# Routed token rows: scattered by expert ahead of time and loaded as whole rows, instead of gathered by an index list

## The reference

```python
def _swiglu(x, w13_, w2_):
    gu = x @ w13_.T
    g, u = jnp.split(gu, 2, axis=-1)
    return jax.nn.silu(g) * u @ w2_.T
scores = jax.nn.softmax(x @ gate_w.T, axis=-1)        # 2048 tokens, 16 experts
topk_w, topk_ids = lax.top_k(scores, 6)
topk_w = topk_w / (topk_w.sum(-1, keepdims=True) + 1e-20)
combine = jnp.einsum('tk,tke->te', topk_w, jax.nn.one_hot(topk_ids, E, dtype=topk_w.dtype))
# out = sum over experts of combine[:, e] * swiglu(x, w13[e], w2[e])  (hidden width 352)
#       + swiglu(x, sw13, sw2)                         (shared, hidden width 704)
x = x + jnp.tanh(g_ffn[0]) * out
```

## Time and profile before

| | |
|---|---|
| median of 3 runs | 1436.95 us (1435.53 to 1438.42) |
| profiled execution: span from first to last instruction | 1435.5 us |
| busy: PE / PEld | 1349.9 us (94%) / 1210.6 us (84%) |
| busy: POOL / DVE / ACT | 949.3 us (66%) / 787.5 us (55%) / 730.9 us (51%) |
| DMA | 149.13 MB, mean 104 GB/s |
| chain that ended last: PE | 65% of the span |
| stage A / shared tiles / routed tiles, about | 0 to 490 / 490 to 700 / 700 to 1425 us |

### The profile page before, as it was taken

How to read it: one execution, slowest core, us unless ns; L and a number is a source line. 1 busy time by engine, 2 the same in 40 slices (tenths; PEclk the granted TensorE clock), 3 DMA queues, 4 the chain that set the end, 5 groups by cost and what they waited for, 6 DMA issues and landing times.

```text
span 1435.5 us, 32257 instructions
## 1 busy us (share of the span) xinstructions
PE 1349.9 (94%) x8480; PEld 1210.6 (84%) x8481; DVE 787.5 (55%) x1364; ACT 730.9 (51%) x1317; POOL 949.3 (66%) x671
## 2 busy tenths in 40 slices
PE   6897998997898899999999999999999999999996
PEld 2686887887888799999998989989889988899885
DVE  6878898898989854653333333333333333333331
ACT  5898897898889464343332333323333333332321
POOL 0588898898988747887456665566645666546632
PEclk8899999999999999999999999999999999999999
DMA  4120122222242365645455435555445544454432
GB/s 137 38 74 31 53 67 96 67 73 91 75 146 72 133 129 106 142 84 141 83 141 145 131 63 144 139 147 137 104 94 137 141 135 104 95 147 131 76 68 36
DMA packets 65042, 149.13 MB, mean 104 GB/s; under 512 B 16976, under 2 KB 17616, under 8 KB 62656
## 3 DMA queue, kind: packets, MB, share of 16 engines
q0 software_dynamic: 31024, 62.10, 22.9%
q1 hardware_dynamic: 33392, 81.21, 17.5%
q10 hardware_dynamic: 560, 4.98, 1.0%
HBM read 101.50 MB, written 48.99 MB: 105 GB/s over the span
## 4 chain that ended last, share of the span: by engine, by line
PE 65%; DVE 3%; issue 1%; POOL 0%; ACT 0%; DVEq 0%; POOLq 0%; ACTq 0%
PE bank L1719 19%; PE bank L1699 19%; PE bank L1700 18%; PE bank L1687 3%; PE bank L1710 3%; DVE hs L1172 1%; PE bank L1604 1%; PE bank L1590 1%; PE bank L1602 0%; POOL hc L949 0%; DVE sc L1226 0%; PE bank L1665 0%; DVEq L1375 0%; DVE xl L1363 0%; DVE du L1186 0%
## 5 line engine op out<-in xcount | busy, mean ns | idle before, releaser
L949 POOL TENSOR_TENSOR hc<-hs,crow 128x512 f32<-128x512 f32 x254 | 322.6, 1302 | 91.8 <-DVE hs L1172 84.6
L1699 PE MATMUL bank<-w,xh 128*128 (+1 forms) x1088 | 368.7, 340 | 7.6 <-issue 4.2
L1015 POOL DMA_INDIRECT out_x<-ys,aid x104 | 171.2, 1646 | 275.0 <-issue 215.7
L1700 PE MATMUL bank<-w,xh 128*128 (+1 forms) x1088 | 351.2, 323 | 0.0
L1172 DVE TENSOR_TENSOR_SCAN hs<-dA,bank 128x512 f32<-128x512 f32 x256 | 295.8, 1208 | 47.9 <-PE bank L1604 32.0
L1719 PE MATMUL bank<-w,ah 128*128 (+1 forms) x816 | 264.7, 405 | 2.7 <-DVE al L1399 2.7
L1399 DVE TENSOR_TENSOR al<-bank,ah 128x384 fp32r<-128x384 f32 x136 | 75.8, 557 | 331.0 <-ACT ah L862 283.2
L1699 PEld LDWEIGHTS bank<-w,xh 128*128 128x128 f32 x1088 | 204.3, 188 | 35.9 <-issue 32.1
L1700 PEld LDWEIGHTS bank<-w,xh 128*128 128x128 f32 x1088 | 206.4, 190 | 2.3
L868 ACT COPY ys<-bank 128x512 f32<-128x512 f32 x136 | 79.9, 587 | 195.9 <-PE bank L1719 191.5
L1700 PE MATMUL bank<-w,xl 128*128 (+1 forms) x544 | 175.9, 323 | 0.0
(11 more groups left out here) (184 smaller groups left out, 2051.7 us busy)
## 6 DMA issues: line engine op xcount, KB each, us to landing
wraw<-in_wall SPq DMA_DIRECT2D x16, 2176.0 KB
crow<-c_rows SPq DMA_DIRECT2D x64, 256.0 KB, 3.3
xt<-token_rows_turned SPq DMA_DIRECT2D x32, 256.0 KB
out_x<-ys POOLq DMA_DIRECT2D x32, 256.0 KB
wraw<-in_wall ACTq DMA_DIRECT2D x2, 2176.0 KB
token_rows<-rowb SPq DMA_DIRECT2D x4, 1028.0 KB
xrow<-in_x SPq DMA_DIRECT2D x4, 1024.0 KB, 7.0
out_x<-xrow SPq DMA_DIRECT2D x4, 1024.0 KB, 4.9
```

The costliest lines, as they stand in the source:

```text
L949: nc.gpsimd.tensor_tensor(hc[:, j, :], hs[:, j, :], crow[:, n % 4, :], ALU.mult).then_inc(hc_done, 1)
L1015: pool.indirect_dma_start(out_rows, bass.IndirectOffsetOnAxis(ap=aid[:, s:s + 1], axis=0), ys[:, s, :], None, bounds_check=TOKENS - 1, oob ...
L1699: nc.tensor.matmul(gate_bank[:, 0:I], xx, columns(w, off + ww + k * 2 * I, I), start=first, stop=last)
L1700: mm = nc.tensor.matmul(up_bank[:, 0:I], xx, columns(w, off + ww + k * 2 * I + I, I), start=first, stop=last)
```

## The change

The token lists and the gathers go. A buffer `expert_rows` in DRAM has a region of 17 x 128 rows for each expert. While the shared tiles run, each batch's finished rows (values, 16 weights, token number, spare) are loaded into SBUF (`srow`, two buffers) and POOL scatters each row of 532 floats to its place in the region of each of its six experts: 96 indirect DMAs, and 16 more that put padding rows behind each expert's last, four a tile in tiles 2 to 29. In the routed stage SP loads each tile as 128 whole neighbouring rows by two DMAs: `xs` (512 values) and `tail` (weights and token number). PE still turns the rows.

SP waits ahead of the first such load for all 112 scatters. SP no longer fetches weights in the routed stage: `wraw` is doubled, and ACT issues the fetch of the set after next right behind its own half of the split, as five DMAs. DVE has no index for the gather to copy, and takes the token number from `tail` instead of from a list by a column number that it first has to load into a register.

```diff
-AHEAD = 5
-FIRST_ROWS = {NS - 3: (NS, NS + 1), NS - 2: (NS + 2,), NS - 1: (NS + 3, NS + 4)}
+TAIL = ROW - H
+IDCOL = TAIL - 2
+REGION = (TT + 1) * P
+PADS = E * REGION
+SCATTERS = TOPK * TT + E
+SCATTERS_AT = dict.fromkeys(range(2, 30), 4)
...
# SP
             def fetch(e):
-                at_least(sp, wl_done, e)
-                sp.dma_start(wraw[:], wall[bass.ds(e, 1)].rearrange("a p c -> p (a c)")).then_inc(raw_in, 16)
+                shared_set(sp, e, raw0)
+
+            def batch_rows(b):
+                if b == 0:
+                    sp.wait_ge(wl_done, 1)
+                if b == 1:
+                    sp.wait_ge(turned_stored, 16 * NB)
+                    sp.wait_ge(base_stored, 16 * NB)
+                sp.wait_ge(rows_stored, 16 * (b + 1))
+                sp.wait_ge(wts_stored, 16 * (b + 1))
+                if b > 1:
+                    sp.wait_ge(listed[b - 2], 16 * TOPK * TC)
+                sp.dma_start(srow[b % 2][:], rows_v[b]).then_inc(srow_in[b % 2], 16)
+
+            def expert_load(t, s):
+                if not (isinstance(t, int) and t < NS + 4):
+                    apart(sp, xt_turned, t - 3, "sp")
+                    apart(sp, aid_done, t - 3, "sp")
+                first = sp.value_load(meta[0:1, 4, bass.ds(t, 1)], min_val=0, max_val=PADS)
+                own = sorted_d[bass.ds(first, P), :]
+                sp.dma_start(xs[:, s, :], own[:, 0:H]).then_inc(expert_in[s], 16)
+                sp.dma_start(tail[:, s, :], own[:, H:ROW]).then_inc(expert_in[s], 16)
...
-            with sp.Fori(3, NX) as e:
-                fetch(e)
             sp.wait_ge(meta_ready, 2)
+            sp.wait_ge(pad_stored, 16)
+            for b in range(NB):
+                sp.wait_ge(listed[b], 16 * TOPK * TC)
+            sp.wait_ge(pads_listed, 16 * E)
+            groups = routed_groups(sp)
+            for k in range(4):
+                expert_load(NS + k, k)
+            with sp.Fori(0, groups - 1) as i:
+                for k in range(4):
+                    expert_load(4 * i + NS + 4 + k, k)
...
# ACT
+            def expert_set(e, at):
+                own = wall[bass.ds(e, 1)].rearrange("a p c -> (a p) c")
+                for k in range(HK):
+                    act.dma_start(wraw[:, bass.ds(at + k * 2 * I, 2 * I)], own[:, k * 2 * I:(k + 1) * 2 * I]).then_inc(raw_in, 16)
+                act.dma_start(wraw[:, bass.ds(at + W2AT, WCOLS - W2AT)], own[:, W2AT:WCOLS]).then_inc(raw_in, 16)
+
+            def fetch_behind(e, t):
+                behind = act.value_load(meta[0:1, 5, bass.ds(t, 1)], min_val=0, max_val=NX - 1)
+                apart(act, wl_done, e, "act")
+                expert_set(behind, raw_at(e + 1))
...
                 with act.If(e > 0):
                     split_high(e, t)
+                    fetch_behind(e, t)
...
# POOL
-            def gather(t, s):
-                ...
-                pool.indirect_dma_start(xt[:, s, :], None, rows_d[:, :],
-                                        bass.IndirectOffsetOnAxis(ap=gid[:, s:s + 1], axis=0)).then_inc(gathered[s], 16)
...
+            def scatter(i):
+                if i < TOPK * TT:
+                    b = i // (TOPK * TC)
+                    if i % (TOPK * TC) == 0:
+                        pool.wait_ge(srow_in[b % 2], 16 * (b // 2 + 1))
+                        pool.wait_ge(pos_ready, b + 1)
+                    pool.indirect_dma_start(sorted_d[:, :], bass.IndirectOffsetOnAxis(ap=posi[:, i:i + 1], axis=0),
+                                            srow[b % 2][:, i % TC, :], None).then_inc(listed[b], 16)
+                else:
+                    e = i - TOPK * TT
+                    if e == 0:
+                        pool.wait_ge(pads_ready, 1)
+                    pool.indirect_dma_start(sorted_d[:, :], bass.IndirectOffsetOnAxis(ap=padi[:, e:e + 1], axis=0),
+                                            padrow[:], None).then_inc(pads_listed, 16)
...
# DVE
-                nc.vector.tensor_copy(aid[:, s4:s4 + 1], lists[:, bass.ds(ids_column(t), 1)]).then_inc(aid_done, 1)
+                nc.vector.tensor_copy(aid[:, s4:s4 + 1], tail[:, s4, IDCOL:IDCOL + 1]).then_inc(aid_done, 1)
...
-                elif gathers:
-                    gather_ids(t + AHEAD, (s4 + 1) % 4)
```

More of the change, by code:

```diff
@@ L513, in tiles_but_12, with raw_here, shared_set, raw_at @@
             return eng.value_load(fours[0:1, 1:2], min_val=NS + E - 12, max_val=TILES - 12)
+        def raw_here(e):
+            return 16 * PARTS * (e + 1)
+        def shared_set(eng, e, to):
+            own = wall[bass.ds(e, 1)].rearrange("a p c -> (a p) c")
+            for k in range(HK + 1):
+                cols = slice(k * 2 * I, (k + 1) * 2 * I if k < HK else WCOLS)
+                eng.dma_start(to[:, cols], own[:, cols]).then_inc(raw_in, 16)
+        def raw_at(e):
+            return ((e + 1) % 2) * WCOLS
         def columns(a, start, size):
@@ L829, in high @@
                 at, size = k * (WCOLS // PIECES), WCOLS // PIECES
[L830 removed]
+                nc.scalar.copy(w[:, at:at + size], raw0[:, at:at + size]).then_inc(*split(0, k, PIECES))
             stage_a(act, ACT_WORK, {"high": high, "setup": setup, "table": exp_and_ln, "rstd": rstd_, "inproj": inproj, "silu": silu, "siluz": siluz, "xproj": xproj, "bt": bt,
@@ L884, in high_piece @@
                 if k == 0:
-                    act.wait_ge(raw_in, 16 * (e + 1))
+                    act.wait_ge(raw_in, raw_here(e))
                     act.wait_ge(down_done, TT * (e - 1))
-                nc.scalar.copy(w[:, base + at:base + at + size], wraw[:, at:at + size]).then_inc(*split(e, k, EARLY))
+                nc.scalar.copy(w[:, base + at:base + at + size], wraw[:, raw_at(e) + at:raw_at(e) + at + size]).then_inc(*split(e, k, EARLY))
             def last_choice(_):
@@ L1069, in _ @@
                     add(t, k)
-            rest = tiles_but_12(pool) + 4
-            for k in range(8):
-                if k + AHEAD < 8:
-                    gather(rest + k + AHEAD, (k + AHEAD) % 4)
-                next_weights(rest + k)
-                expert_starts(rest + k, k % 4)
-                add(rest + k, k % 4)
         @block.vector
@@ L1447, in beside, with tile @@
                         fill_table(i)
-            def tile(t, s4, gathers=False, adds=False, m=None):
+            def tile(t, s4, adds=False, m=None):
                 s = s4 % 2
@@ L1454, in tile @@
                     beside(DVE_AFTER_A, t)
-                if isinstance(t, int) and t < NS:
-                    for late in FIRST_ROWS.get(t, ()):
-                        gather_ids(late, late % 4)
-                elif gathers:
-                    gather_ids(t + AHEAD, (s4 + 1) % 4)
                 x_low(t + 1, 1 - s)
```

199 lines of the change are left out of this document (103 added, 96 removed).

## The result

| | before | after |
|---|---|---|
| median of runs on one chip | 1437.68 us (1435.53 to 1441.47, 4 runs) | 1482.21 us (1481.86 to 1484.03, 4 runs) |
| ratio, 95% interval | | 1.0309 [1.0292, 1.0327] |
| profiled execution: span | 1435.5 us | 1480.3 us |
| PE busy | 1349.9 us (94%) | 1359.0 us (92%) |
| POOL / DVE busy | 949.3 / 787.5 us | 849.9 / 750.5 us |

The changed kernel is 3.1% slower. The forecast was 1466 us, in a range of 1444 to 1488: sign and range hold, and the likeliest value is 16 us short. POOL and DVE have 99 and 37 us less to do, as the diff promised, and nothing of it reaches the end.

A forecast was written before the change was run, and what follows sets the result against it. PE, busy 94% of the span, was taken to bound the kernel. 1435.5 + 17.7 (seam) + 11.4 (expert changes) = 1464.6 us for the profiled execution, 1466 for the median, which lies 1.45 higher; range 1444 to 1488.

The forecast's parts named there:

- What bounds the kernel: Whole kernel: PE, busy 94%; in the routed stage all other engines together cost PE only 19.1 us.
- Part 1, the seam: Between shared and routed tiles: PE stands 15.7 us for SP's wait, plus 2 for low clock; 17.7 us (10.4 to 30).
- Part 2, DMA: Beside the shared tiles: DMA engines about 1.0 busy, a backlog of a few us, no stall of PE before the seam.
- rival B: Beside the shared tiles: DMA engines don't keep up, 12 to 36 us on top, 1478 to 1502, say 1484; chance 0.20.
- Part 3, expert changes: At 15 expert changes: ACT's issues delay `ah` and `down`, 1.05 less 0.29, net 0.76 each, 11.4 us (-8.4 to +18).
- The credit of 0.29 a change for `gid`: At expert changes: without `gid` on DVE, PE's 0.29 us wait for `xl` goes; gain 0.29 to 0.56 each.
- The ordinary tiles and POOL: Routed stage: DVE's lighter work in ordinary tiles and POOL's 104 fewer gathers gain nothing.
- rival D: Routed stage: its 19.1 us loss goes entirely, seam at its lower bound; 1426.8, with the offset 1428; chance 0.08.
- rival C: At expert changes: ACT's issues are hidden, the seam costs as forecast; 1448.8, with the offset 1450; chance 0.20.

The follow-up runs named there:

- Experiment 3: Changed kernel, SP waiting before the first four row loads only for token rows and the padding of the first four experts: 1469.6 us, ratio 1.0229.
- experiment 1: Changed kernel with each weight set fetched by one DMA instead of five: 1455.4 us, ratio 1.0141.
- experiment 5: Changed kernel with each weight set fetched by three DMAs instead of five: 1465.2 us, ratio 1.0192.
- experiment 8: Changed kernel with fetch issues on SP and first loads early, but the second register load and its wait back on ACT: 1438.9 us, ratio 1.0008.
- experiment 11: Changed kernel with 3200 of the 4352 columns of a set's rounding copy on DVE instead of 2176: 1483.5 us, ratio 1.0313.
- Experiment 6: Changed kernel with fetch on SP and first loads early, plus the `gid` register load and copy back on DVE: 1441.0 us, ratio 1.0018.
- experiment 7: Changed kernel with fetch on SP and first loads early, plus 3200 of the copy's 4352 columns on DVE instead of 2176: 1433.2 us, ratio 0.9969.
- experiment 9: Kernel before, without the change, with 3200 of the copy's 4352 columns on DVE instead of 2176: 1429.1 us, ratio 0.9931.

## Why the prediction was right and wrong

- **What bounds the kernel**: right. PE's own work did not change (the routed tiles that are neither change nor next take 6.83 us before and 6.84 after, on average), and all that was lost was lost at the seam and at 15 expert changes.
- **Part 1, the seam**: right in mechanism and nearly in size, 14.6 for 17.7. POOL's last issue ended at 700.4 (701.5 forecast). The landing took 1.9 us from there, not 5.5: the 4 us added for whole rows queued ahead would have fitted the scatters of the full stretch (5.0 and 4.0 from the start of the issue), but not the last, which took 2.84. SP took 1.96 (2.1), the second load went 0.57 later (0.4), and landed in 2.3 (3.3). PE turned at 707.31 where 712.8 was forecast. With the 1.9 us in front, and by the timeline of both (696.95 before), this is 12.3 later instead of 15.7. The low clock came as forecast: from the start of the turning to the end of `down` 5.04 us passed instead of 2.69, so 2.3 more for the 2 forecast. 12.3 and 2.3 are the 14.6. Experiment 3 takes away 12.7 of it.
- **Part 2, DMA**: right. "About 1.0" was 0.97, with no stall in the tiles before the seam, so rival B, with its 12 to 36 us, fails.
- **Part 3, expert changes**: this is the mis-sized term, 32.0 us for 11.4. The mechanism was the one named, `ah` and then `down` behind ACT's issues (experiments 1, 5, 8 and 11). Its size was wrong even by the prediction's own upper bound, 18 us. An issue took 0.53 us from start to start, not 0.40: the DMA instruction itself takes 0.35, close to SP's 0.33, but in front of most stand two more instructions and gaps:

```profile
L920 ACTq DMA_DIRECT2D wraw<-in_wall x68: 347/349/639, 583.6 to 1384.2; - x68
L920 ACTq FUSED_REGOPS  x60: 64/69/124, 721.3 to 1384.1; - x60
L920 ACTq MOVE wraw<-in_wall x60: 29/29/29, 721.5 to 1384.2; - x60
```

  In a typical change the five took 2.51 us for the 2.00 forecast, the copy was dispatched 0.16 later behind `ys` (1.24 against 1.08), 0.10 passed from the last issue to `ah`, and the register load was right (1.00 for 1.07). So `ah` was 1.85 us later than before (4.85 against 3.00), not 1.15. The credit of 0.29 a change for `gid`, 4.4 us in all, did not come: the tiles behind take the same, 7.43 and 7.37. Such a change lost 1.77 us (8.68 against 6.91), 26.5 over 15, where 0.76 was forecast for each. The remaining 5.5 us the prediction had put at nothing. In four changes the loop's branch came on top; by the one that kept its full clock (9.32) that is 0.64 each, 2.6 us. In three of these the clock fell and took about 3.1 more; I had counted a clock only at the seam.
- **The credit itself** was a wrong reading of the earlier trace rows. I took the releaser of a 0.29 us gap as its cause and did not look at why all of that tile was late. Experiment 6 shows that it was not `gid`, experiments 7 and 9 that it was, for the greater part, `ah` behind the copy.
- **The ordinary tiles and POOL**: right, nothing gained from 99 us less on POOL, so rival D fails with its 19 us. In rival C the issues are hidden; that is what the kernel with one DMA does: its routed stage loses nothing, and its 1455 lies above C's 1450 mostly by the 4.4 us for `gid` that C still counted.

By the parts as measured, 1435.5 - 1.9 + 14.6 + 32.0 = 1480.2, against a span of 1480.3. That the time fell into the range was in part luck: Part 3 came out at nearly three times its forecast, and the room for it had been made for a later seam and for rival B, neither of which came.

## What to carry to other kernels

Count a train of DMA issues as work of its engine, at the pitch seen between issues with run-time addresses and not at the length of one instruction, and ask what is queued behind the last of them: here five issues in front of one short copy, and what followed from them, cost 32 us over 15 changes; the same five on an idle queue cost nothing. Look at more than one case, too: the change read above for its match with the earlier trace rows is one of the four slow ones, and only a typical one beside it shows the loop's branch. Before a short wait is put down to the releaser that a row names, look whether that releaser was done early, and what made the whole tile late; the row behind the gap may show the last event and not the cause. A wait for "all written" at the seam of two stages can often be cut to what the first loads need, which here gave back 12.7 of 14.6 us.

## What the runs showed of the hardware

- DMA engines were busy 0.97 of the time for 178 us, at 289 GB/s, without PE losing anything; here a shared tile's rows were loaded three tiles ahead, and an adding had four tiles until its buffer was written again. Scatters of 128 rows of 2128 bytes took 5.0 us (median) from the start of their issue to landing, the last, with none behind it, 2.84.
- In the changed kernel the granted clock fell to its lower level (1.2 GHz) at three of the four expert changes where PE had waited 2.12 to 2.25 us, and at none of the eleven with 1.43 to 1.83. This is no sharp line: it also fell once behind 1.78 us in the kernel with the first loads early and once in the changed kernel with the copy shared 3200, and at the seam of kernel 7 behind two gaps of 1.14 and 0.71. With three DMAs (waits up to 1.13) it fell at no expert change.
- An indirect scatter of 128 rows of 2128 bytes took POOL 1.06 us to issue on average (0.97 for the padding rows), that of 128 elements of 4 bytes 1.07: no cost of the row's size shows.
- At the end of a turn of ACT's loop the branch put 0.4 us more between the last DMA issue and the next compute instruction (0.51 against 0.10). Under a running copy of 2 us, as in the kernel before, such a branch cost nothing that shows.
